# Windowed attention in a long transformer kernel: numerators and denominators of a head from one 128-column product

## What is computed

```python
q = l2norm(q) * qs
k = l2norm(k) * ksc
q, k = rotary_xpos(q, k)
...
sim = jnp.einsum('bhwid,bhwjd->bhwij', bq, bk)
mask = (i < j) | (i > j + WINDOW) | (j == -1)
sim = jnp.where(mask, -jnp.finfo(sim.dtype).max, sim)
attn = jax.nn.softmax(sim, axis=-1)
out = jnp.einsum('bhwij,bhwjd->bhwid', attn, bv)
...
x = x + o @ wo
```

## Time and profile before

| | us |
|---|---|
| median of 3 runs | 6118.09 (6118.06 to 6119.7) |
| the profiled execution, its own time | 6125.03 |
| its span in the profile | 6123.2 |
| one windowed-attention stage, four in the program | about 427 |
| ten steady trips inside the first of them | 251.2 |

### The profile page before, as it was taken

One profiled execution on the slowest core, in us unless ns is written; L12 is line 12 of the kernel. 1 busy time (PEld: TensorE's weight loads), 2 busy tenths in 40 slices (PEclk: granted clock), 3 DMA queues, 4 the chain that ended last, 5 costly groups with the idle time before them and its releaser, 6 DMA issues. The chain is left out here.

```text
span 6123.2 us, 113557 instructions
## 1 busy us (share of the span) xinstructions
PE 5316.8 (87%) x39222; PEld 2810.7 (46%) x39222; DVE 3563.9 (58%) x4189; ACT 3332.0 (54%) x4968; POOL 2568.9 (42%) x1902
## 2 busy tenths in 40 slices
PE   5866888888888998999897999899897999787999
PEld 2322555555544554554343554555343444343443
DVE  4757999999964553554354554554554343554444
ACT  4745888888854553554454554455354333443343
POOL 1333999999943662663133662664231000000000
PEclk8986999999999999999898999999899999888999
DMA  1002111111110110110000110111000210001111
GB/s 43 17 10 83 31 31 32 32 30 31 31 52 24 43 43 10 42 42 19 4 15 25 42 42 14 42 41 28 28 15 20 55 41 14 0 0 28 38 33 28
DMA packets 143957, 182.98 MB, mean 30 GB/s; under 512 B 33584, under 2 KB 86960, under 8 KB 142512
## 3 DMA queue, kind: packets, MB, share of 16 engines
q1 hardware_dynamic: 143792, 180.85, 11.1%
HBM read 80.31 MB, written 12.85 MB: 15 GB/s over the span
## 5 line engine op out<-in xcount | busy, mean ns | idle before, releaser
L2502 POOL TENSOR_TENSOR arena<-arena,wbig 128x1024 f32<-128x1024 f32 x512 | 1191.4, 2472 | 107.7 <-ACT arena L2438 107.6
L2489 DVE TENSOR_TENSOR_SCAN arena<-banks,arena 128x1024 f32<-128x1024 f32 x512 | 1140.6, 2278 | 68.4 <-ACT banks L2433 49.4
L963 ACT ACTIVATE arena<-banks,wbig 128x512 f32<-128x512 f32 x512 | 351.8, 687 | 591.2 <-PE banks L921 582.5
L1020 DVE TENSOR_TENSOR arena<-arena 128x512 f32<-128x512 f32 x512 | 353.2, 692 | 470.7 <-ACT arena L963 436.4
L2433 ACT ACTIVATE banks<-banks 128x1020 f32<-128x1020 f32 x512 | 518.1, 1012 | 108.5 <-PE banks L2354 100.9
L1510 POOL TENSOR_TENSOR arena<-arena 128x512 f32<-128x512 f32 x256 | 354.9, 1386 | 527.3 <-DMA arena<-arena 527.3
L635 DVE TENSOR_REDUCE arena<-banks 128x4 f32<-128x1024 f32 (+1 forms) x384 | 401.7, 1046 | 280.0 <-PE banks L462 225.7
L2438 ACT COPY arena<-banks 128x1024 f32<-128x1024 f32 x512 | 520.8, 1017 | 51.2 <-POOL arena L2502 29.9
L571 ACT ACTIVATE Y<-banks 128x2048 f32<-128x2048 f32 x192 | 305.6, 1592 | 306.4 <-PE banks L498 236.4
L931 PE MATMUL banks<-arena,wbig 128*128 128x512 f32 x1024 | 463.5, 598 | 0.0
L921 PE MATMUL banks<-Z,wbig 128*128 x1024 | 459.1, 593 | 0.0
(11 more groups left out here) (304 smaller groups left out, 9887.0 us busy)
## 6 DMA issues: line engine op xcount, KB each, us to landing
arena<-arena SPq DMA_DIRECT2D x1024, 64.0 KB, 2.0
arena<-scratch_g SPq DMA_DIRECT2D x64, 512.0 KB, 10.8
wbig<-wbig SPq DMA_DIRECT2D x48, 240.0 KB, 3.1
wbig<-scratch_d SPq DMA_DIRECT2D x512, 16.0 KB, 1.7
wbig<-scratch_b SPq DMA_DIRECT2D x64, 128.0 KB, 2.2
wbig<-scratch_c SPq DMA_DIRECT2D x64, 128.0 KB, 2.1
arena<-Z SPq DMA_DIRECT2D x64, 128.0 KB, 2.1
wbig<-in_l_ffn SPq DMA_DIRECT2D x1, 4197.0 KB, 12.4
```

What stands on the lines that cost most here:

```text
L963: act.activation(hid[e % 2][:, f, :], hbank[f], ACT.Relu, bias=b1[:, e, f:f + 1])\
L1020: last = dve.tensor_tensor(hid[e % 2][:, f, :], hid[e % 2][:, f, :], gate[u][:, e, :], ALU.mult)
L2489: dve.tensor_tensor_scan(own, line(decay_bank[n % 2]), own, 0.0, ALU.mult, ALU.add)\
L2502: pool.tensor_tensor(four(h[par][:, m * 1024:m * 1024 + 1024]), four(us[n % 2]), Bs[par].unsqueeze(1).to_broadcast([128, 4, SEQ]), ALU.mult)\
```

## The change

`v` gets a third slot: for each of the two chunks of 128 tokens and each group, 64 columns of head 0's values, 64 columns of ones, 64 columns of head 1's values. The ones are written once per stage. Head 0 takes the first 128 columns as weights (values, then ones), head 1 the last 128 (ones, then values). One product gives 64 rows of numerators and 64 rows of denominators; head 0 writes them to columns 0 to 255 of the bank, head 1 to columns 256 to 511. Head 0's denominators thus stand in rows 64 to 127, head 1's in rows 0 to 63, each in the half opposite to its numerators. `Ln` becomes two instructions of 64 rows, each reading one half and writing the other; `normalize` becomes two of 64 rows as well.

```diff
-    v = [take(2 * 512).rearrange("p (c h d) -> p c h d", c=2, h=WHEADS) for _ in range(2)]
+    v = [take(2 * 4 * 192).rearrange("p (c f s d) -> p c f s d", c=2, f=4, s=3) for _ in range(2)]
...
             dve.memset(mx, 0.0).then_inc(cleared.sem, 1)
+            for par in range(2):
+                dve.memset(v[par][:, :, :, 1, :], 1.0).then_inc(cleared.sem, 1)
...
-            dve.wait_ge(cleared.sem, cleared.at(5))
+            dve.wait_ge(cleared.sem, cleared.at(7))
...
                 for c, at, n, first in ((0, 0, 192, 0), (1, 192, 128, 128)):
                     for r in range(2):
-                        pe.matmul(to[half_rows(r), first:first + n], v[par][:, c, 2 * f + r, :],
-                                  prob[f % 2][:, r, at:at + n], start=(c == 0), stop=True, skip_group_check=True)
-                for c, at, n, first in ((0, 0, 192, 0), (1, 192, 128, 128)):
-                    for r in range(2):
-                        last = pe.matmul(to[half_rows(r), SEQ + first:SEQ + first + n], ones[:, 0:WDIM],
-                                         prob[f % 2][:, r, at:at + n], start=False, stop=True, skip_group_check=True)
+                        last = pe.matmul(to[:, r * SEQ + first:r * SEQ + first + n],
+                                         v[par][:, c, f, r:r + 2, :].rearrange("p s d -> p (s d)"),
+                                         prob[f % 2][:, r, at:at + n], start=(c == 0 and r == 0), stop=True,
+                                         skip_group_check=True)
                 last.then_inc(pe_o.sem, 1)
...
-                    last = act.copy(v[par][:, c, :, :].rearrange("p h d -> p (h d)"), bank[c])
+                    last = act.copy(v[par][:, c, :, 0:3:2, :], bank[c].rearrange("p (f r d) -> p f r d", f=4, r=2))
...
-                act.activation(recip[f % 2], obank[f % 2][:, SEQ:2 * SEQ], ACT.Ln).then_inc(act_d.sem, 1)
+                for r in range(2):
+                    last = act.activation(recip[f % 2][half_rows(r), :], obank[f % 2][half_rows(1 - r), r * SEQ:(r + 1) * SEQ],
+                                          ACT.Ln)
+                last.then_inc(act_d.sem, 1)
...
-                dve.tensor_tensor(oT[:, f, :], obank[f % 2][:, 0:SEQ], recip[f % 2], ALU.mult).then_inc(dve_n.sem, 1)
+                for r in range(2):
+                    last = dve.tensor_tensor(oT[half_rows(r), f, :], obank[f % 2][half_rows(r), r * SEQ:(r + 1) * SEQ],
+                                             recip[f % 2][half_rows(r), :], ALU.mult)
+                last.then_inc(dve_n.sem, 1)
```

More of the change, by code:

```diff
@@ L1122, in window_attention_stage @@
     obank = [k.psum[:, 6 + n, :] for n in range(2)]
-    cleared = Count(k, "cleared", 5)
+    cleared = Count(k, "cleared", 7)
     ones = k.c["ones"]
```

## The result

The changed kernel takes 6163.24 us (median of 5 runs, 6152.75 to 6174.77) against 6119.7 (5 runs, 6118.06 to 6122.79) before: ratio 1.0074, interval 1.0063 to 1.0085. It is 43.5 us slower, outside the range of 6112 to 6152.

What follows compares the result with a forecast made beforehand. Bound: a ring through TensorE, ScalarE, swap DMAs and GpSimd, with TensorE waiting 0.70 us per trip for `low`. 56 trips x 0.05 = 2.8, plus 3.2 memsets and 4.3 tails: +10.3 us, 6128 from a median of 6118.1; range 6112 to 6152.

Steps and rivals of the forecast that it cites:

- Bound and ring: Steady trips, 25.12 us: a ring through TensorE, ScalarE's `copy_raw(0)`, swap DMAs and GpSimd's `sin0` to `low0` sets the period.
- TensorE: `values`: each passage between halved and full array costs about 0.10 and an uncovered load 0.05; the change loses both passages.
- `project(0)` is then ready at -0.18: TensorE on the ring: `turn(1)` starts 0.18 us earlier, limited by `reduce`, and `project(0)` is ready as much earlier.
- ScalarE: Second `Ln` changes halves, so +0.39 us; with -0.15 from TensorE and 0.19 to spare, `copy_raw(0)` comes at +0.05.
- VectorE: `normalize` becomes two instructions, the second held a full 0.43 and the next operation 0.09 later: +0.53 us each, taken as hidden.
- The step that failed: VectorE beside GpSimd: `cosine` 2 starts at 2072.30 instead of 2072.10, before `add1` at 2072.53, so GpSimd's chain stays.
- The lost turn: Rival: `cosine` 2 comes after `add1` has started and waits it out; about 0.9 us per trip, 6178 us; chance 0.08.
- Ends: Stage starts and last trips: two memsets 0.80 us per stage, 3.2 for four; tails about +1.1 per stage, 4.3 in all.

Runs made afterwards that it cites:

- e2: Changed kernel with `normalize` as one 128-row instruction again (head 1 gets wrong numbers): 6140.49 us, ratio 1.0035.
- e5: Changed kernel with `values_in` moved ahead of `exponential(0)` on ScalarE: 6147.89 us, ratio 1.0053.
- e3: Kernel before the change with one more 128 x 256 VectorE product ahead of `normalize(0)` in every trip: 6131.41 us, ratio 1.0018.
- e6: Changed kernel with `cosine` 2 moved ahead of `normalize(0)` on VectorE: 6137.32 us, ratio 1.0033.
- e4: Kernel before the change with two more 128 x 256 VectorE products ahead of `normalize(0)` in every trip: 6266.93 us, ratio 1.0249.
- e12: Changed kernel with one 128-row scaled copy for the two `Ln` and one 128-row `normalize` (wrong values): 6121.95 us, ratio 1.0006.
- e14: Changed kernel with `cosine` 0, 1 ahead of `copy_raw(3)`, 2, 3 ahead of `normalize(0)`, and one 128-row `normalize` (head 1 wrong): 6072.92 us, ratio 0.9925.
- e15: Changed kernel with `cosine` 0, 1 ahead of `copy_raw(3)`, 2, 3 ahead of `normalize(0)`, and one 128-row scaled copy for both `Ln`: 6065.49 us, ratio 0.9913.
- e1: Changed kernel with one 128-row scaled copy in place of the two `Ln` (logarithm left out): 6182.44 us, ratio 1.0106.
- e7: Changed kernel with `cosine` 0 and 1 moved ahead of `copy_raw(3)` on VectorE: 6175.72 us, ratio 1.0102.

## Why the prediction was wrong

- *Bound and ring*: right. Trips of 25.12 come back in e2, and what lengthens `low0` lengthens the trip.
- *TensorE*, -0.10 and -0.05 at each passage: right. "`project(0)` is then ready at -0.18" failed: it is held by `values_in`, whose end no step of mine looked at. e5 gives back about 0.1. `normalize(0)` came 0.19 sooner after `sin0`, not 0.38.
- *ScalarE*, second `Ln` +0.39 and `copy_raw(0)` +0.05: right (8.45 for 8.43, so +0.02).
- *VectorE*, +0.53 for the second `normalize`: near. The second half starts 0.43 after the first, and the next operation comes 0.89 after `normalize` starts (0.87 put). This agrees with what I cited from the Trainium skill, "VectorE: DVE Perf Modes", "Two Vector instructions with no wait between them": the second starts 0.43 after the first, when that is over.
- **The step that failed**: "It must still come before `add1`, now at 2072.53; 0.23 to spare, so GpSimd's chain stays." The limit is not `add1`'s start but 4.65 us after `sin0`, 0.69 before the end that `cosine` 2 had anyway. A misreading stands behind it: I wrote that `add0` finishes 1.27 after `cosine` 1, as if each took its whole turn, and did not hold the same measure against `add1`. It is 1.13 for both, and it says that `add1`'s end was tied to `cosine` 2 already. Before, 0.08 to 0.18 was to spare. At my own 4.72 to 4.77 the trip would already have grown by about 0.1. At the measured 4.80 to 4.92 it grew by 0.16 to 0.27. Over 52 steady periods the four stages' values sum to 13 x (0.27 + 0.16 + 0.20 + 0.21 + 4 x 0.02) = 12 us, and with the two lost turns 22 of the 23. That it comes so near is in part luck: the 2.6 us of the trip of 27.71 are not in it, and the sum is 1.3 too high in the last two stages. e3 shows this without the change, e2 and e6 take it away.
- *The lost turn*, given 0.08 and 0.9 us per trip, did come, in two trips of the profiled execution, and cost 5.0 us each. The mechanism is the rival's, the size was missing the clock: a trip behind 2.00 us of idle TensorE runs 10.3 us at half clock. Where the clock stays up a lost turn costs 0.5 (e4), not 0.9. That the number of such trips differs between executions would explain why the changed kernel's runs lie 22 us apart and those of before 5; this is not shown, since only one execution was profiled.
- *Ends*: 3.2 for the memsets measured 4.4: the instruction behind them starts 1.27 us after the first memset (1905.21 to 1906.48), 0.19 in the earlier trace rows, 1.08 later and not 0.80. The 0.08 of overlap that I took off each memset was not there. Tails of "+1.1 per stage, 4.3 in all" measured 9.3: the terms of the chain were right (2.34 for 1.39 before the last `mix`), and the fourth tail, at full clock, grew by 1.2; but in three stages the last `mix` fell to half clock, 1.6 us in the row above. The first two trips (+3.6) had no term; from the memset to the third `sin0` TensorE's granted clock was half for 102 us in the four stages, 84 before. e2 and e12 show such trips too, and which wait sets it off is not traced.

## What to carry

When two engines take turns, read an operation's margin from its end: it is how much later it may start before that end moves, and not the distance to the other engine's next start. Add what different engines lose along each chain instead of judging it piece by piece: with the `cosine`s moved each doubling alone was free in the trips (e14, e15) and both together were not, and with the old order the doubled `normalize` alone cost 60 us (e1 against e12). And look at the order of work before removing any: moving four `cosine`s into VectorE's idle time gave 0.7% of the time, with nothing removed.

## What the runs showed of the hardware beyond that

- A 512-column VectorE product of 0.69 us with both inputs in SBUF takes 0.77 to 1.81 beside GpSimd's of 1.27, and GpSimd's up to 1.82, by who starts first; a start difference of 0.01 us (2152.17 and 2152.18) decided 5 us. The Trainium skill, "GPSIMD Engine Reference", "Specifications", names the contention with VectorE instructions of two SBUF inputs; the traces agree, and show it as whole instructions in turn.
- TensorE's granted clock fell to half behind idle stretches of 2.00 us and of 2.34 us (after), but not behind each of a length. Counted by trips with a lost turn it fell behind 10 of 47 of 1.2 us (e7), 31 of 49 of 1.6 us (e4) and 11 of 14 of 2.0 us (after and e1); behind 2.34 us it fell in three of four stages. Behind the 0.9 us of every steady trip after it stayed full.
- ScalarE too holds a second instruction that changes the half of the rows: 0.39 us from start to start for two `Ln` of 64 rows, 0.77 for both, against 0.38 for one of 128.
